# Layer 1's key tiles of 384 and 128 queries share a step; gates are copied out of the side bank, VectorE's branch moves, and the end runs in halves

## The reference

```python
# layer 0: 16 heads of 8, all 1024 keys
q, k = l2norm(x @ Wq), l2norm(x @ Wk)          # over the 128 channels
out = softmax(q k^T / sqrt(8)^2 / temperature) v ;  x = LN(x + out @ proj + b)
x = LN(x + quantized_matmul(x))                # rows rounded to int8
# layer 1: layernorm of each head of q and k, rope, causal mask
out = softmax(mask(q k^T / sqrt(8))) v ;  x = LN(x + out @ Wo + bo)
h = silu(x @ Wgate^T) * (x @ Wup^T) ;  x = LN(x + h @ Wdown^T)     # hidden 384
```

## Time and profile before

| what | value |
|---|---|
| median of 3 runs | 943.94 us (940.53 to 944.69) |
| the profiled execution, its own time | 944.33 us |
| its span, first to last instruction | 942.5 us |
| PE busy | 868.2 us (92%) |
| ACT busy | 795.9 us (84%) |
| DVE busy | 562.9 us (60%) |
| POOL busy | 155.3 us (16%) |
| chain that ended last, by engine | PE 65%, DVE 16%, ACT 12%, issue 5% |
| mean granted clock of PE | 0.957 of full speed |

### The profile page before, as it was taken

The page is one execution under the profiler, slowest core; times in us unless marked ns, Lnnn a source line. Parts: engine busy times, 40 slices in busy tenths (PEclk is TensorE's granted clock), DMA queues, the critical chain, the costliest instruction groups (busy, mean ns, idle before and its releaser), DMA issues.

```text
span 942.5 us, 16640 instructions
## 1 busy us (share of the span) xinstructions
PE 868.2 (92%) x6210; PEld 305.3 (32%) x6210; DVE 562.9 (60%) x1583; ACT 795.9 (84%) x958; POOL 155.3 (16%) x352
## 2 busy tenths in 40 slices
PE   7799999999998999999999999999999898999973
PEld 3233322323233323333323332333323333433333
DVE  5365556866887776587623677367622666644446
ACT  4599999989997899888898799898899888878840
POOL 3000000000004200133001500023000622342210
PEclk9599999999999899999899899999999999979987
DMA  5545314116135223323411311421401321331000
GB/s 160 199 164 186 128 37 154 45 66 226 56 113 180 68 68 124 128 75 107 152 44 56 114 45 50 142 79 34 157 23 46 101 68 45 132 111 39 1 23 13
DMA packets 48551, 88.60 MB, mean 94 GB/s; under 512 B 5073, under 2 KB 14417, under 8 KB 48465
## 3 DMA queue, kind: packets, MB, share of 16 engines
q1 hardware_dynamic: 47984, 87.00, 27.2%
q10 hardware_dynamic: 480, 0.48, 0.2%
HBM read 51.03 MB, written 35.65 MB: 92 GB/s over the span
## 4 chain that ended last, share of the span: by engine, by line
PE 65%; DVE 16%; ACT 12%; issue 5%; POOL 1%; DMA 0%; DVEq 0%; SPq 0%; ACTq 0%; POOLq 0%
PE ps L825 31%; PE ps L805 18%; ACT probs L702 12%; PE ps L775 4%; PE ps L782 3%; PE ps L724 3%; PE ps L786 2%; PE ps L760 2%; DVE mid_sq L1028 1%; DVE mid_st L1030 1%; POOL probs L618 1%; DVE mid_part L1199 1%; DVE mid_part L1198 1%; DVE mid_qk L1060 1%; DVE mid_st L328 1%
## 5 line engine op out<-in xcount | busy, mean ns | idle before, releaser
L702 ACT ACTIVATE probs<-ps 128x1024 f32<-128x1024 f32 (+3 forms) x896 | 775.0, 946 | 93.2 <-PE ps L825 49.6
L825 PE MATMUL ps<-probs,v_st 128*32 128x512 f32 (+3 forms) x3584 | 449.1, 574 | 12.3 <-issue 6.3
L805 PE MATMUL ps<-q_st,k_st 32*128 32x512 f32 (+3 forms) x1792 | 297.4, 479 | 24.2 <-ACT probs L702 18.5
L805 PEld LDWEIGHTS ps<-q_st,k_st 32*128 32x128 f32 x1792 | 126.7, 185 | 316.0 <-ACT probs L702 212.1
L618 POOL TENSOR_SCALAR_AFFINE_SELECT probs<-probs 128x256 f32<-128x256 f32 x256 | 112.6, 450 | 262.4 <-ACT probs L702 260.0
L825 PEld LDWEIGHTS ps<-probs,v_st 128*32 128x32 f32 x3584 | 72.0, 109 | 122.7 <-issue 93.2
L601 POOL COPY v_st<-v_all 128x256 f32<-128x256 f32 (+1 forms) x65 | 28.9, 446 | 335.2 <-PE ps L825 327.5
L1213 DVE TENSOR_TENSOR last_y<-ps,last_y 128x128 f32<-128x128 f32 x24 | 7.0, 292 | 60.9 <-PE ps L786 60.7
L1209 DVE SCALAR_TENSOR_TENSOR hT<-ps,th 128x512 f32<-128x512 f32 x21 | 14.5, 692 | 48.2 <-PE ps L782 48.2
L1185 DVE COPY mid_qkv<-ps 128x384 f32<-128x384 f32 x32 | 17.8, 558 | 34.9 <-PE ps L775 34.1
L1074 DVE STREAM_TRANSPOSE sums_t<-ps 128x512 f32<-128x512 f32 x32 | 22.9, 717 | 25.8 <-PE ps L825 24.6
(11 more groups left out here) (161 smaller groups left out, 633.0 us busy)
## 6 DMA issues: line engine op xcount, KB each, us to landing
k_st<-parts_scratch SPq DMA_DIRECT2D x47, 512.0 KB, 3.6
parts_scratch<-mid_part SPq DMA_DIRECT2D x36, 512.0 KB, 3.9
q_st<-parts_scratch SPq DMA_DIRECT2D x63, 256.0 KB, 4.0
parts_scratch<-prep_part SPq DMA_DIRECT2D x28, 512.0 KB, 4.1
k_st<-parts_scratch SPq DMA_DIRECT2D x16, 256.0 KB, 2.8
xT<-in_xT SPq DMA_DIRECT2D x8, 256.0 KB, 4.9
x_all<-in_x SPq DMA_DIRECT2D x8, 256.0 KB, 5.3
out<-yo SPq DMA_DIRECT2D x8, 256.0 KB, 2.3
```

Source lines behind the costliest of these rows:

```text
L702: nc.scalar.activation(probs[:, k % PS, :, 0:w], slot(k)[:, :, 0:w], ACT.Exp).then_inc(probs_ready, 1)
L805: last_ = mm(slot(k)[:, e, 0:w], k_st[row, p % KB, kt * P:(kt + 1) * P], q_st[row, p % KB, lo:HALF], start=True, stop=not shifted)
L825: last_ = mm(acc[HR * h:HR * (h + 1), lo:HALF], v_st[:, p % VB, kt, h, :], probs[:, (2 * s + h // 2) % PS, h % 2, 0:w], start=first and p ...
```

## The change

1. **Steps.** `pass_steps` now gives steps of several tiles. Odd chunks of layer 1 take (0), (6), (1), (5, 7), (2), (4), (3), even ones (0), (2), (1, 3): the tile of 384 queries and that of 128 share one slot, one exponential of 1024 and one turn of the loop. Their matmuls stay the same in number and size, POOL masks each of the two. 416 steps instead of 448.
2. **Gates.** VectorE copies a gate from the side bank to `gate_sb` and so releases it; ACT takes the tanh from there, in its queue after the exponentials of two steps later (`TANH_AT`); the unit `up` now does both multiplications, and the order is gate 0, gate 1, up 0, gate 2, up 1, up 2. `held` is gone.
3. **Planner.** Layer 1's feed-forward is due 26 steps after its start instead of 32; before a turn no unit of VectorE is planned that would run past it; a step of n tiles is modelled for PE as 0.3 + 0.15 n + 1.1 of its width.
4. **Start.** VectorE reads `FIRST_KEYS` ahead of its branch; no other unit is planned before step 7 (`BRANCHED`). Pass 1's rows are loaded ahead of the store of the second chunk's queries, for which q and k have semaphores of their own. PE runs 22 instead of 15 empty matmuls while it waits for the first rows, and 3 more in each of the steps 0 and 1.
5. **End.** A written-out `end()` takes the place of `END_ORDER`: turn, projection, residual and layernorm in halves of 256 tokens into banks of their own, ACT copies the high part of the transposed tokens, gates begin with it, the down matmuls go by hidden tile as each is ready, the output is stored in halves, and empty matmuls (`HOLD`) fill PE's waits. VectorE's left-over units of chunk 6 (`LEFT`) stand between the low part and the gates.

The core of the diff:

```diff
 def pass_steps(layer, qh):
+    kts = [(kt,) for kt in range(KT)]
     if layer:
-        kts = [0, 7, 1, 6, 2, 5, 3, 4] if qh else [0, 3, 1, 2]
+        kts = [(0,), (6,), (1,), (5, 7), (2,), (4,), (3,)] if qh else [(0,), (2,), (1, 3)]
...
 def pe_time(s):
-    return 0.45 + 1.1 * STEPS[s][3] / HALF
+    return 0.3 + 0.15 * len(STEPS[s][1]) + 1.1 * STEPS[s][2] / HALF
...
-        jobs.append(dict(name="last", c=c, after=after, due=min(after + 32, NS)))
-    jobs.append(dict(name="consts", c=0, after=3, due=16))
+        jobs.append(dict(name="last", c=c, after=after, due=min(after + 26, NS - 6)))
+    jobs.append(dict(name="consts", c=0, after=BRANCHED, due=16))
...
-                if e != "dve" or dve > at[min(s + 2, NS + 2)] + 0.4:
+                if e != "dve" or dve > at[min(s + 2, NS + 2)] + 0.4 or s + 1 in sum_turns and dve + cost > at[s + 2] + 0.4:
                     break
...
         def tanh(c, j):
-            act.wait_ge(side_filled, FILL["last", c, "gate", j] + 1)
-            nc.scalar.activation(th[:], side, ACT.Tanh, scale=0.5 / 127).then_inc(tanh_ready, 1)
+            act.wait_ge(gate_copied, c * NJ + j + 1)
+            nc.scalar.activation(th[:, j % 2, :], gate_sb[:, j % 2, :], ACT.Tanh, scale=0.5 / 127).then_inc(tanh_ready, 1)
...
             elif what == "gate":
-                dve.wait_ge(tanh_ready, c * NJ + (k + 1))
-                stt(out=th[:], in0=th[:], scalar=1.0, in1=side, op0=ALU.add,
-                    op1=ALU.mult).then_inc(side_read, 1)
+                v.tensor_copy(gate_sb[:, k % 2, :], side).then_inc(side_read, 1)
                 got()
+                dve.sem_inc(gate_copied, 1)
             elif what == "up":
+                dve.wait_ge(tanh_ready, c * NJ + (k + 1))
+                chain[lane(name, c)].link(stt(out=th[:, k % 2, :], in0=th[:, k % 2, :], scalar=1.0, in1=gate_sb[:, k % 2, :], op0=ALU.add, op1=ALU.mult))
...
+        units(FIRST_KEYS)
         far_scores = dve.value_load(far_any[0:1, 0:1], min_val=0, max_val=1)
 
         def steps(shifted):
-            if shifted:
-                units(FIRST_KEYS)
...
+        def end():          # TensorE
+            pe.wait_ge(probs_ready, 2 * NS)
+            hold(HOLD[0])
+            pe.wait_ge(side_read, len(FILL))
+            for h in range(2):
+                pe.wait_ge(end_attn, h + 1)
+                for t in range(2 * h, 2 * h + 2):
+                    last_ = mm(ps[:, PROJ_BANK[h], t % 2 * P:(t % 2 + 1) * P], attn[:, t * P:(t + 1) * P], w_out[:, 1, :],
+                               start=True, stop=True)
+                last_.then_inc(end_proj, 1)
+            hold(HOLD[1])
```

More of the change, by code:

```diff
@@ L274, in slot_of @@
                 return s
-    return -1 if name == "prep" and c < 2 else NS + 1 + [(x[0], x[1], x[3], x[4]) for x in END_ORDER].index((name, c, what, k)) / 1000
+    assert (name, c) in (("prep", 0), ("prep", 1), ("last", NCH - 1)) or (name, c, "dve", what, k) in LEFT, (name, c, what, k)
+    return -1 if name == "prep" else NS + 1
 def check_order():
@@ L288, in check_order @@
     assert outs == sorted(outs), outs
-    assert not any(x[3] == "turn" for x in END_ORDER)
 check_order()
@@ L480, in load_rows @@
             layer, b, qh, g = PASSES[p]
-            sp.wait_ge(parts_out[layer_job[layer]], 16 * NOUT * chunks_needed(layer, b, qh))
+            for u in range(2):
+                sp.wait_ge(parts_out[layer_job[layer]][u], 16 * PARTS * (1 if p == 1 and u == 0 else chunks_needed(layer, b, qh)))
             if p >= KB:
@@ new lines, in end @@
+            hold(HOLD[1])
+            for t in range(TC):
+                pe.wait_ge(end_norm, t + 1)
+                last_ = tp(ps[:, TURN_BANK[t // 2], t % 2 * P:(t % 2 + 1) * P], tok["last"]["y1"][:, t, :], ident[:])
+                if t % 2:
+                    last_.then_inc(end_turned, 1)
+            hold(HOLD[2])
+            part = lambda u, j, n: mm(ps[:, 2 * j + u, :], w_hid[:, u, j * P:(j + 1) * P], yTp[:, n, :],
+                                      start=(n == 0), stop=(n == PARTS - 1))
@@ L1272, in steps @@
                             shifts(p)
-                units([x for x in SIDE_ORDER[s] if not (shifted and x in FIRST_KEYS)])
-            units(END_ORDER)
+                units([x for x in SIDE_ORDER[s] if x not in FIRST_KEYS])
+            end()
         counted = {n: ch.n for n, ch in chain.items()}
```

275 lines of the change are left out of this document (156 added, 119 removed).

## The result

The changed kernel takes 893.7 us (median of 4 runs, 892.65 to 898.33), the kernel before in the same measurement 943.33 us: ratio 0.9487, 95% interval 0.9446 to 0.9528, so 49.6 us less. The prediction had 904 us, 39.3 us less than the 943.33 measured beside it. It was right in its sign and its range (884 to 927), and 10.3 us too careful. The profiled execution took 892.65 us, its span is 890.9 us, and PE's mean granted clock is 0.994 where it was 0.957.

The account below looks back on a forecast made before the run. ACT and PE run in lockstep, each making the other wait, between a start and an end held by VectorE. Terms -8 - 6 - 12 - 7.6 + 3 - 9 = -39.6 us gave 904 us; 8 in 10 range 884 to 927.

Parts of the forecast that it names:

- start: Up to about 44 us: VectorE reading the keys before its branch saves 8 us, bounds 3 and 10.
- shared steps: Layer 1: 32 fewer steps save fixed costs of ACT and PE, 6 us, from 0 to 13.4.
- turns: Middle: VectorE's late turns of the sums stall PE and lower its clock; three places at 4 us, 12 us saved, 0 to 20.
- gates, with the copies: Middle: half of ACT's 15.2 us of tanh waits goes, -7.6 us; VectorE's 21 copies cost +3 us.
- end: After the last exponential: halves, order and full clock shorten VectorE's chain by 9 us, bounds 5 and 11.
- fourth slow place: Middle: one of four low places in the clock line; only three, which begin with PE's sums waiting, were priced.
- second rival: Start: the keys' DMA takes over and fights with the stores, so the start gives only 3 us: 909 us; chance 0.12.
- fourth rival: Gates: `up` starves the bank, PE waits behind two multiplications and loses its clock; slower than before, up to 967 us; chance 0.04.
- nothing is in between: End: the last sums no longer stand behind down units and the last tile is unmasked: 1.2 us, gain 1.2.
- at full clock, 4.7: End: from the turned sums to the normalized tokens 4.7 us instead of 6.5, with halves side by side; gain 1.8.
- the middle gives nothing: Middle: PE is the bound with the same matmuls, so only start and end gain: 927 us; chance 0.25.
- More than the sum: Layer 1: narrow steps make ACT and PE wait for each other and both waits go: 882 us; chance 0.1.

Follow-up runs that it names:

- experiment 6: The changed kernel with VectorE's reads of `FIRST_KEYS` behind its branch again, as before the change: 901.05 us.
- experiment 1: The changed kernel with one key tile in each step again, in the old order of the tiles: 905.66 us.
- experiment 3: The changed kernel without the planner's rule that keeps VectorE's units from running past a turn of the sums: 902.5 us.
- experiment 4: The changed kernel without the gate copy: tanh, one step after the gate, and VectorE's multiplication read the side bank, on the same plan: 899.94 us.
- experiment 9: The changed kernel with single tiles in the old order and without the planner's turn rule: 910.52 us.
- 10: The changed kernel without the 45 empty matmuls of its end (`HOLD` all zero): 894.11 us.
- 11: The changed kernel with pass 1's queries loaded ahead of its keys: 892.19 us.
- 12: The changed kernel with pass 1's queries loaded first, four more empty matmuls before PE's wait for these rows, and chunk 6's output moved behind the last normalization: 892.04 us.

## Why the prediction was right, point by point

The sign, the range and the mechanisms held; the sizes did not in three terms, and one of them, the shared steps, was half of what was measured. Each term against what stands behind it:

| term | predicted | measured | by what |
|---|---|---|---|
| start | -8 | -7.4; -10.4 at the twelfth exponential | experiment 6; timeline |
| shared steps | -6 | -12.0 | experiment 1 |
| turns | -12 | -8.8 | experiment 3 |
| gates, with the copies | -4.6 | -6.2 | experiment 4 |
| end | -9 | -5.6 | timeline |
| sum | -39.6 | -40.0 | |

**That the five parts add up to the predicted sum is chance.** Errors of 0.6, -6.0, 3.2, -1.6 and 3.4 us nearly cancel, and the five parts explain 40.0 of 49.6 us. 9.6 us are attributed to no part by an experiment, and 13.6 if shared steps and turns are taken together (16.8 us in experiment 9). Left for them are what no run undid alone: `held`, the due times, the order gate 0, gate 1, up 0, the model of PE, and the interplay of these. Experiment 9 shows where much of it lies: in layer 0, where no step is shared, and in the fourth slow place, which the prediction saw in the earlier trace rows and gave no price. It also says that it isn't the interplay of shared steps and turns. On the kernel before the parts gave 11 us for turns and 18.6 for shared steps, but those intervals (6 to 12, 10 to 22) hold the 8.8 and 12.0 us as well. More than that stays open.

**Start.** Right, with the mechanism as told: the DMA took 6.65 us from VectorE's read to PE instead of 7.1. Of the earlier trace rows's 11.7 us, 10.4 went. Pass 1's rows are late next, as the second rival had it for the DMA; but by the profiled starts it costs some 4.5 us in some executions and nothing in others, so that rival came true in part of them.

**Shared steps: the term that was sized wrong.** The prediction put it as "0.15 for the sums and half of the 0.42 for the scores, some 0.3 us in each of 32 steps". The 0.15 was exact. The scores' 0.42 us are no sum over the two pairs, which run side by side: six matmuls take 0.44 us where four or two take 0.43, so the whole group goes, not half of it. It then took 6 of 9.6 us, "since either engine is the bound in its part of the time". Where no slow place disturbs the comparison, experiment 1 has the full saving of PE, 0.52 us in the clean even chunk and 0.49 to 0.75 in three odd ones; the 12.0 us are what the slow places on either side leave of it. The rule cited from the Trainium skill (TensorE: Matmul & The Clock Gate, Wait — 56ns, not 53.3ns?) made the saving almost nothing for PE; the trace does not agree, since the same work takes 1.44 us in one turn and 1.99 in two. Most of that difference is the group of scores.

**Turns.** Right in kind: after, the waits and the 1.94 us sums of the earlier trace rows are gone, and without the rule two of them return. Alone on the kernel before it removes two of three in the profiled execution. "Three places at 4 us" was too dear: experiment 3 has one place of 5.7 us and one of 1.3. Between the first projection and the last two short stretches at the lower clock are left after. One is at 504 to 508 us in the second even chunk, which takes 24.3 us with it and 23.2 in the traces of experiments 4, 10, 11 and 12 without it. The other begins at a shared step:

```profile
742.43 0.62 POOL L602 COPY v_all<-mid_qkv 128x512 f32<-128x512 f32 x1 [5.37 <-DVEq L1243]
...
743.00 3.19 POOL L625 TENSOR_SCALAR_AFFINE_SELECT probs<-probs 128x256 f32<-128x256 f32 x6
...
745.52 1.07 PE L857 MATMUL ps<-probs,v_st 128*32 128x384 f32 x16 [1.82 <-POOL probs L625]
...
747.11 1.94 PE L857 MATMUL ps<-probs,v_st 128*32 128x512 f32 x8
```

POOL stood 5.37 us at a copy that VectorE had to release; six masks were queued behind it, and the sums of a shared step need two of them for each pair. The prediction passed over that with "the sums wait for them one turn later, as before". PE stood 1.82 us, and the eight sums after it took 1.94 us. The price can be estimated from experiment 1, where this chunk is free of it: it is 1.7 us shorter than after, the other three odd ones are 2.0 to 3.0 longer, so the place costs some 4 us.

**Gates.** Gain and cost together came out about right (-6.2 measured for the pair, -4.6 predicted); no run has them apart. Nearly half of the 15.2 us goes without the copy, in the new steps and plan (8.5 left in experiment 4). The risk lay elsewhere than the fourth rival said: not at `up`, where PE's weight loads wait at most 0.8 us for the copy, but in the tanh, which costs 23.4 us when it is one step too early.

**End.** 5.6 of 9 us. The pieces of the projection and the gates are as forecast; missing are the three pieces of chunk 6 named above, 0.87 + 1.0 + 1.16 = 3.0 us, which the prediction had called "nothing is in between" and "a gap of about 1.1 us". Two of them came from the plan, which leaves a down unit and a layernorm for the last steps. The empty matmuls, part of "at full clock, 4.7", gave 0.4 us that can't be told from nothing.

**What the prediction wanted to see.** There are 832 exponentials, the tanh's wait is gone, the wait for the sums is "well under 49.6" (32.4), the clock line has no low slice, and the first run of exponentials (eight, then a gap of 0.47 us) begins at 31.0 instead of 36. Two of its marks failed. From the last exponential to the end are 29.1 us and not 25.5. And of the even chunks, of which it said that 24 us or more would make it wrong, two still take 24.8 and 24.3 (30.9 and 26.5 before) and a third 23.95 (30.2), and only the clean one 22.0; all four are faster by 2.1 to 6.3 us all the same, so the mark was set too low.

**The rivals.** That the middle gives nothing (0.25) is out: 38.8 us of the gain lie between the first projection and the last (5.1 + 16.6 + 17.1). More than the sum (0.1, at 882 us) pointed the right way, though no run tests its reason, narrow steps that make PE and ScalarE wait for each other, apart from the steps' own cost; 893.7 lies between it and the forecast, inside the forecast's own 893 to 917 by a hair.

## What to carry to other kernels

Where a matmul engine works in small groups between waits, price a merged step by the groups that vanish, not by all their columns: read the pitch of a group at two widths and at two counts, since matmuls in different rows of the array go side by side. And count what the merged step newly waits for. A copy that frees a bank early pays only if its reader on the next engine is queued late enough that it never waits for the copy; try the two places in the queue together. And in a tail that one engine's small instructions rule, what counts is every left-over unit on that engine; empty matmuls beside it were worth 0.4 us here, no more than the noise.

## What the runs showed of the hardware

- Score matmuls (32 rows deep) of two pairs of heads go side by side here: two, four or six of them take 0.42 to 0.44 us from start to start where the wider pair has 512 columns, and four take 0.37 us where it has 384. 16 sums of 384 and 128 columns take 1.00 us, where two groups of eight took 1.15.
- At pass 1's rows, behind waits of 0.60, 0.68, 0.75 and 0.91 us PE's next group ran at the higher clock (0.50 us); behind waits of 1.55, 1.95, 2.36, 2.37 and 3.22 us the same group took 0.79 or 0.80 us. Elsewhere the wait alone doesn't decide: behind 1.89 us (experiment 3, 300.25) eight sums took 1.07 us, behind 1.07 us (441.80) 1.94.
- At its read of the flag and its branch VectorE stood idle for 7.17 us before and 7.83 us in experiment 6, with nothing to wait for. After, the branch lies inside an idle time of 11.36 us.
- The same single tiles in the order 0, 6, 1, 5, 7, 2, 4, 3 took 12 us more than in the order 0, 7, 1, 6, 2, 5, 3, 4, and 13.3 us more in the odd chunks alone.
- A lower clock at the end (4.55 instead of 3.02 us for twelve matmuls) lengthened it by 0.1 us (23.2 instead of 23.1), which is nothing that can be told.
